# A three-layer compressed interaction network on one core: first layer's sums on ScalarE, first loads on two queues, squares first

## The reference, cut to what matters

```python
e = jnp.stack([tbl_f[ids[:, f]] for f in range(32)], axis=1)     # (2048, 32, 16)
x0, xk, outs = e, e, []
for W in (W0, W1, W2):                                           # (32, Hk, 64), Hk = 32, 64, 64
    xk = relu(einsum('bmd,bhd,mhk->bkd', x0, xk, W))
    outs.append(sum(xk, axis=2))                                 # over d, 16 wide
z = concatenate(outs, axis=1)                                    # (2048, 192)
h = relu(concatenate([z, dense_ctx], 1) @ W_top1 + b_top1)       # 208 -> 512
h = relu(h @ W_top2 + b_top2)                                    # 512 -> 256
y = h @ W_top3                                                   # 256 -> 1
```

## Time and profile before

| | us |
|---|---|
| median of 3 runs | 1193.18 (1192.31 to 1193.81) |
| the profiled execution | 1192.97 |
| its span, first to last instruction | 1191.2 |
| busy: PE / DVE / POOL / ACT | 1121.3 / 1118.8 / 918.8 / 733.9 |
| PE idle at L600, ended by DVE's first-layer products (L556) | 41.6 |
| PE idle at L600, ended by DVE's products (L516) | 21.8 |
| mean time of an `xb` relu (L317), an output relu (L357), a sum (L543) | 0.564, 0.598, 0.776 |

### The profile page before, as it was taken

One profiled execution on the slowest core, in us unless ns is written; L12 is line 12 of the kernel. 1 busy time (PEld: TensorE's weight loads), 2 busy tenths in 40 slices (PEclk: granted clock), 3 DMA queues, 4 the chain that ended last, 5 costly groups with the idle time before them and its releaser, 6 DMA issues.

```text
span 1191.2 us, 14658 instructions
## 1 busy us (share of the span) xinstructions
PE 1121.3 (94%) x5312; PEld 393.6 (33%) x5312; DVE 1118.8 (94%) x521; ACT 733.9 (62%) x1361; POOL 918.8 (77%) x640
## 2 busy tenths in 40 slices
PE   0488899999999999999999999999999999999997
PEld 0122223333333333333333333333333333333333
DVE  0487999999999999999999999999999999999995
ACT  0343666676667667665766766576676657657653
POOL 6688888888888888888888888888888888885400
PEclk9888999999999999999999999999999999999999
DMA  5887787667678766677876666788666778876300
GB/s 110 190 176 146 158 171 155 138 132 144 140 157 171 157 141 141 132 144 150 172 163 136 143 134 145 144 171 168 139 140 134 143 145 169 166 144 144 61 1 1
DMA packets 76216, 167.25 MB, mean 140 GB/s; under 512 B 21776, under 2 KB 39072, under 8 KB 76144
## 3 DMA queue, kind: packets, MB, share of 16 engines
q1 hardware_dynamic: 59216, 161.95, 64.8%
q0 software_dynamic: 16384, 4.23, 3.6%
q10 hardware_dynamic: 544, 0.14, 0.1%
HBM read 157.86 MB, written 8.40 MB: 140 GB/s over the span
## 4 chain that ended last, share of the span: by engine, by line
PE 86%; POOL 3%; DVE 3%; DMA 3%; issue 3%; ACT 1%; SPq 1%; DVEq 0%
PE acc L600 80%; POOL x_rows L254 3%; DVE p_dve L516 3%; PE acc L672 3%; PE acc L658 1%; PE acc L660 1%; DMA q_tile<-x_of_steps 1%; ACT xb L317 1%; DMA x_rows<-in_table,ids_s 1%; PE acc L680 1%; DMA spread<-x_of_steps 1%; SPq L192 1%; DMA x_of_steps<-x_rows 0%; SPq L219 0%; DVE z L543 0%
## 5 line engine op out<-in xcount | busy, mean ns | idle before, releaser
L600 PE MATMUL acc<-p_dve,w_s 128*64 128x512 f32 x3840 | 863.2, 598 | 22.5 <-DVE p_dve L516 21.8
L254 POOL DMA_INDIRECT x_rows<-in_table,ids_s x512 | 493.7, 964 | 146.1 <-issue 131.2
L516 DVE TENSOR_TENSOR p_dve<-spread,xb 128x3072 f32<-128x3072 f32 (+2 forms) x224 | 572.2, 2682 | 2.9 <-issue 2.9
L516 DVE TENSOR_TENSOR p_dve<-spread,xa 128x2048 f32<-128x2048 f32 (+1 forms) x192 | 501.5, 2730 | 16.6 <-issue 9.1
L600 PEld LDWEIGHTS acc<-p_dve,w_s 128*64 128x64 f32 x3840 | 267.9, 137 | 571.5 <-issue 467.2
L317 ACT ACTIVATE xb<-acc 32x512 f32<-32x512 f32 x512 | 288.8, 564 | 71.6 <-DVE p_dve L516 65.5
L266 POOL TENSOR_TENSOR p_l<-spread,q_tile 128x2048 f32<-128x2048 f32 x60 | 272.7, 4573 | 11.0 <-DMA q_tile<-x_of_steps 10.4
L308 ACT ACTIVATE xa<-acc 64x512 f32<-64x512 f32 x256 | 145.9, 570 | 189.6 <-PE acc L600 155.0
L277 POOL TENSOR_TENSOR p_pool<-spread,x_s 128x1024 f32<-128x1024 f32 x64 | 152.2, 2378 | 94.7 <-PE acc L600 45.9
L600 PE MATMUL acc<-p_l,w_s 128*64 128x512 f32 (+1 forms) x640 | 152.5, 612 | 41.6 <-DVE p_l L556 41.6
L326 ACT ACTIVATE x_s<-acc 64x512 f32<-64x512 f32 x256 | 151.5, 592 | 8.3 <-ACT y_row L449 4.8
(11 more groups left out here) (18 smaller groups left out, 151.1 us busy)
## 6 DMA issues: line engine op xcount, KB each, us to landing
spread<-x_of_steps SPq DMA_DIRECT2D x248, 512.0 KB, 17.4
q_tile<-x_of_steps SPq DMA_DIRECT2D x128, 128.0 KB, 11.4
x_rows<-in_table,ids_s POOLq DMA_INDIRECT x512
x_of_steps<-x_rows SPq DMA_DIRECT2D x64, 128.0 KB
spread<-x_of_steps SPq DMA_DIRECT2D x16, 256.0 KB, 5.4
w_s<-in_w SPq DMA_DIRECT2D x2, 512.0 KB, 5.7
wt<-in_w_top SPq DMA_DIRECT2D x1, 512.0 KB, 6.5
z_all<-in_dense_t ACTq DMA_DIRECT2D x16, 8.0 KB, 8.2
```

Of the source, the lines that this page charges most:

```text
L254: nc.gpsimd.indirect_dma_start(out=x_rows[:, s % 2, i * DIM:(i + 1) * DIM], out_offset=None, in_=table, in_offset=bass.IndirectOffsetOnAxi ...
L516: nc.vector.tensor_tensor(p_dve[:, to:to + n, :], spread[:, s % 3, tile:tile + n, :], over(x[:], n), ALU.mult).then_inc(dve_made, n)
L600: last = nc.tensor.matmul(acc[b * K:(b + 1) * K, :], w, prod[:, b * BLK:(b + 1) * BLK], start=start, stop=stop)
```

## The change

1. `out_0` and VectorE's sum of the first layer go. In their place `sums_0` on ScalarE reads acc0 in 32 ACTIVATEs of 128 x 16, each with an accumulator output that is the sum over d, written to `z`. It stands behind x1_b(s). The waits of TensorE for `out_ready[0]` become waits for `z_made[0]`.
2. In steps 0 and 1 `load_q` and `load_a` are shared: SP issues quads 0 and 1, ScalarE quads 2 and 3 (`load_q_and_a`), tile by tile, each tile with its own semaphore. Step 0's `load_b` is shared too; step 1's isn't. VectorE makes those steps' first-layer products in four instructions of one chunk. ScalarE issues step 0's before squares(0) and step 1's behind x1_b(0), ahead of sums_0(0).
3. TensorE's first layer begins with the squares' chunk.
4. out_2(s - 2) comes after x2_a(s - 1). squares(2) comes after x2_b(0) instead of before it.
5. mlp1 and mlp2 come after chunk 8 instead of chunk 5 of layer 1.

```diff
-MLP1_AFTER, MLP2_AFTER, MLP3_AFTER = 5, 5, 13
+MLP1_AFTER, MLP2_AFTER, MLP3_AFTER = 8, 8, 13
...
                 if s < 2:
-                    load_tiles(s, 0, NA // 2, half_a_loaded[s])
-                    load_tiles(s, NA // 2, NA - NA // 2, a_loaded[s])
+                    for i in range(NA - 1):
+                        load_tiles(s, i, 1, tile_loaded[s][i], SP_QUADS)
+                    load_tiles(s, NA - 1, 1, a_loaded[s], SP_QUADS)
...
-                load_tiles(s, NA, NT - NA, b_loaded[s % 3])
+                load_tiles(s, NA, NT - NA, b_loaded[s % 3], SP_QUADS if s == 0 else range(Q))
...
-            def out_0(s):
+            def sums_0(s):
                 if s > 0:
                     act.wait_ge(z_made[0], s)
-                nc.scalar.activation(out_l[:, 0, :], acc0[:], ACT.Relu).then_inc(out_ready[0], 1)
+                if s % 2 == 0 and s >= 4:
+                    act.wait_ge(z_moved, s // 2 - 1)
+                for i in range(SB // 2):
+                    cols = slice(i * DIM, (i + 1) * DIM)
+                    last = nc.scalar.activation(out_l[:, 0, cols], acc0[:, cols], ACT.Relu,
+                                                accum_out=z[:, s // 2 % 2, 0, s % 2, i:i + 1])
+                last.then_inc(z_made[0], 1)
...
+            def load_q_and_a(s):
+                act.wait_ge(x_stored, 32 * (s + 1))
+                if s >= 1:
+                    act.wait_ge(l0_made, CP * s)
+                    act.wait_ge(squares_made, s)
+                for q in ACT_QUADS:
+                    act.dma_start(q_tile[q * FIELDS:(q + 1) * FIELDS, :],
+                                  scratch[s, 0:FIELDS, :]).then_inc(q_loaded, 16)
+                for i in range(NA - 1):
+                    load_tiles(s, i, 1, tile_loaded[s][i])
+                load_tiles(s, NA - 1, 1, a_loaded[s])
             load_dense(0)
+            load_q_and_a(0)
+            load_tiles(0, NA, NT - NA, b_loaded[0])
             act.wait_ge(w_loaded, LOADED)
             squares(0)
             x1_a(0)
             x1_s(0)
-            out_0(0)
             for s in range(STEPS):
...
                 x1_b(s)
+                if s == 0:
+                    load_q_and_a(1)
+                sums_0(s)
+                if s >= 1:
+                    x2_a(s - 1)
                 if s >= 2:
                     out_2(s - 2)
-                if s >= 1:
-                    x2_a(s - 1)
-                if s + 1 < STEPS:
+                if s != 1 and s + 1 < STEPS:
                     squares(s + 1)
...
                     x2_b(s - 1)
+                if s == 1:
+                    squares(2)
...
                     x1_s(s + 1)
-                    out_0(s + 1)
...
-                for c in 0, 2:
-                    if c == 2:
+                for c in range(CP):
+                    if c < CP - 1:
+                        dve.wait_ge(tile_loaded[s][c], 16 * Q)
+                    else:
                         dve.wait_ge(a_loaded[s], 16 * Q)
-                    nc.vector.tensor_tensor(p_l0[:, c:c + 2, :], spread[:, s % 3, c:c + 2, :],
-                                            over(q_tile[:], 2), ALU.mult).then_inc(l0_made, 2)
+                    nc.vector.tensor_tensor(p_l0[:, c, :], spread[:, s, c, :], q_tile[:],
+                                            ALU.mult).then_inc(l0_made, 1)
...
                     if c == NT:
-                        sums(s, 0)
...
-                for c in range(C0):
+                for c in CP, *range(CP):
                     rows = P if c < CP else FIELDS
-                    if c == 0 and s > 0:
+                    if c == CP and s > 0:
                         pe.wait_ge(x1b_ready, s)
-                        pe.wait_ge(out_ready[0], s)
+                        pe.wait_ge(z_made[0], s)
```

More of the change, by code:

```diff
@@ L32 @@
 RING = 10
+SP_QUADS, ACT_QUADS = (0, 1), (2, 3)
 H1, H2 = 512, 256
@@ L137, in build_kernel @@
         q_loaded = sem("q_loaded")
-        half_a_loaded = [sem(f"half_a{s}_loaded") for s in range(2)]
+        tile_loaded = [[sem(f"tile{i}_of_step{s}_loaded") for i in range(NA - 1)] for s in range(2)]
         a_loaded = [sem(f"a_loaded{u}") for u in range(3)]
@@ L153, in build_kernel @@
         x2b_ready = sem("x2b_ready")
-        out_ready = [sem(f"out{n}_ready") for n in range(3)]
+        out_ready = [sem(f"out{n}_ready") for n in (1, 2)]
         z_made = [sem(f"z{n}_made") for n in range(3)]
@@ L184, in store_x, with load_tiles @@
                     sp.dma_start(dst, x_rows[:, s % 2, :]).then_inc(x_stored, 16)
-            def load_tiles(s, first_tile, n, signal):
-                for q in range(Q):
+            def load_tiles(s, first_tile, n, signal, quads=range(Q)):
+                for q in quads:
                     o = Q * first_tile + q + 1
@@ L217, in load_q @@
                     sp.wait_ge(squares_made, s)
-                for q in range(Q):
+                for q in SP_QUADS if s < 2 else range(Q):
                     sp.dma_start(q_tile[q * FIELDS:(q + 1) * FIELDS, :],
@@ L451, in mlp3, with load_tiles @@
                 act.dma_start(y[:, t * P:(t + 1) * P], y_row[:]).then_inc(y_stored, 16)
+            def load_tiles(s, first_tile, n, signal):
+                for q in ACT_QUADS:
+                    o = Q * first_tile + q + 1
+                    first = scratch[s, o:o + 1, :]
+                    src = bass.AP(first.tensor, first.offset, [[COLS, FIELDS], [Q * COLS, n], [1, COLS]])
+                    act.dma_start(spread[q * FIELDS:(q + 1) * FIELDS, s, first_tile:first_tile + n, :],
+                                  src).then_inc(signal, 16)
+            def load_q_and_a(s):
[3 more added lines that the diff above has]
+                    act.wait_ge(squares_made, s)
+                for q in ACT_QUADS:
+                    act.dma_start(q_tile[q * FIELDS:(q + 1) * FIELDS, :],
[3 more added lines that the diff above has]
+                load_tiles(s, NA - 1, 1, a_loaded[s])
             load_dense(0)
+            load_q_and_a(0)
+            load_tiles(0, NA, NT - NA, b_loaded[0])
             act.wait_ge(w_loaded, LOADED)
@@ L616, in layer0 @@
                         pe.wait_ge(squares_made, s + 1)
-                    contract(acc0, w0_s[0:rows, c, :], p_l0[0:rows, c, :], c == 0, c == C0 - 1
+                    contract(acc0, w0_s[0:rows, c, :], p_l0[0:rows, c, :], c == CP, c == CP - 1
                              ).then_inc(l0_used, 1)
@@ L622, in layer1 @@
                 if c == 0 and s >= 2:
[L623 removed]
+                    pe.wait_ge(out_ready[0], s - 1)
                 if c != POOL_CHUNK:
@@ L636, in layer2 @@
                 if c == 0 and s > 0:
-                    pe.wait_ge(out_ready[2], s)
+                    pe.wait_ge(out_ready[1], s)
                 if c != POOL_CHUNK:
```

12 lines of the change are left out of this document (5 added, 7 removed).

## The result

The changed kernel takes **1381.68 us** (median of 4 runs, 1380.26 to 1382.62), the kernel before 1192.74 (4 runs). The ratio is 1.158, 95% interval [1.156, 1.160]: slower by 189 us, where 11.8 less were forecast, and far outside the range.

What follows compares the result with a forecast made beforehand. DVE was taken to set the step, with PE balanced against it from step 4 on. Terms 7.9 + 1.2 + 2.0 + 0.7 = 11.8 us gave 1181.4 on the median's scale; range 1176 to 1200, the forecast's own 1177 to 1187.

Steps and rivals of the forecast that it cites:

- 16 columns come to 0.22 us: ScalarE's sums_0: each 16-column accumulating ACTIVATE takes 0.22 us, bounds 0.07 and 0.44, so 7.0 us for the 32.
- with 7.0 nothing waits: TensorE's mlp1 and mlp2 leave sums_0 7.8 us, so a row of 7.0 us delays nothing.
- Rival A: sums_0 holds PE over acc0; each microsecond beyond 7.8 lengthens 28 steps: 1205, 1231 or far above; chance 0.20.
- the forecast's case: The main forecast for the whole kernel: 11.8 us gained, 1181.4 on the scale of the median; chance 0.56.
- First steps: Steps 0 and 1, up to DVE's layer 1 of step 2: start at 112.2 instead of 120.06, 7.9 us gained.
- which POOL's gathers set and which stays within 0.7 us: Step 1's loads: they start when the gathered rows are stored, 54.81, a time expected to move by 0.7 us at most.
- Steps 2 and 3: No top network yet, PE has room: DVE's dropped sum saves 0.6 us in each, 1.2 us.
- From step 4 on: PE is the bound; only its 0.18 us wait per two steps goes: 2.0 us taken, bounds 0 and 2.5.
- Rival C: DVE alone was the bound: 0.6 us saved in each of 28 steps, 17 us, giving 1166; chance 0.03.
- The tail: At the end DVE is ahead, so its wait at 1153.17 goes: 0.7 us gained.
- Rival B: Early loads arrive no earlier, since half-size DMAs on two queues share engines: 8.3 us gained, 1184.7; chance 0.17.
- Rival D: A small stall, 0.25 to 0.26 us per ACTIVATE, or an early-step wait that eats the gain: about 1192; chance 0.04.

Runs made afterwards that it cites:

- h1: The changed kernel, unaltered, measured again and undisturbed: 1177.55 us, ratio 0.9876 against the kernel before.
- e2: The changed kernel with 32 plain 16-column ACTIVATEs (no accumulator output) and DVE doing the first-layer sum again, undisturbed: 1203.94 us, ratio 1.0096.
- i1: The changed kernel, unaltered, on another chip, undisturbed: 1178.23 us, ratio 0.9884.
- e1: The changed kernel with one ScalarE relu of acc0 in place of sums_0 and DVE's first-layer sum back, undisturbed: 1186.88 us, ratio 0.9954.
- j3: The kernel before with only the loads of steps 0 and 1 on two queues, disturbed chip: 1195.34 us, ratio 1.0016.
- k3: The changed kernel without the gathers of steps 6 to 31, disturbed chip: 1208.37 us, ratio 1.0141.
- k2: The changed kernel with acc0 first copied to SBUF by one relu, TensorE waiting for that alone, sums reading the copy, disturbed chip: 1289.12 us, ratio 1.0796.
- k1: The changed kernel, unaltered, as control on a disturbed chip: 1380.14 us, ratio 1.1578.
- e4: The changed kernel with acc0 first copied to SBUF by one relu, TensorE waiting for that alone, sums reading the copy, undisturbed: 1177.48 us, ratio 0.9872.
- j1: The changed kernel, unaltered, a fourth time, disturbed: 1375.49 us, ratio 1.1532.

## Why the prediction was wrong, and where it was right

**The step that failed is "16 columns come to 0.22 us"**, 7.0 us for the 32, and with it "with 7.0 nothing waits". The price of a row of 32 was taken as a property of the instructions. It is one as long as they arrive: a pair takes 0.157 us, 5.4 or 5.5 us for 32 (h1), below the forecast 7.0. With gathers running beside them on a disturbed chip the same 64 take 9.5 to 12.2 us in the steps 2 to 29 of the three traces, 11.8 on the mean in the trace on record, or 0.37 for each ACTIVATE. That still lies between the prediction's own bounds, 0.07 and 0.44, but 0.44 was meant for a slower instruction, and the range was worked out with 0.22. No instruction became slower: the median ACTIVATE of the row lasts 185 ns in the trace on record and 292 in h1. What was added is time between them, and the longest row of small ACTIVATEs that the prediction had was the six z_all.

**Rival A's mechanism is what happened.** It said that sums_0 would hold TensorE over acc0 beyond 7.8 us, and that PE would be idle before mlp1 and mlp2. In h1 the limit measures 7.7: sums at 628.63, mlp2 at 636.29. A priced each microsecond beyond it at 28 steps; 26 of them have a long row, 11.8 us on the mean, and that is 4.0 x 26 = 104 us, or 1285. The rest up to 1382 has two large parts that A lacked: TensorE's slow pace after each wait (1.7 + 0.55 us in the step shown; with the wait of 4.3 it makes 6.5, and the step grew from 34.5 to 41.0), and the first steps, 16 us later than before instead of 8 earlier, in which sums of 19.6 and 15.8 us and the late issues on SP add up. The range ended at A's beginning, 1200, though A's own numbers went to 1231 and "far above". With a chance of 0.20 for a rival without an upper end, that was the wrong place to cut.

The Trainium skill's page "VectorE: DVE Perf Modes", section "Two Vector instructions with no wait between them", was weighed for A: on VectorE an accumulator output makes two instructions. The trace agrees, and shows it for ScalarE as well: 1024 ACTIVATE and 1024 ACTIVATION_READ_ACCUMULATOR. That doubling costs 0.157 - 0.065 = 0.09 us for each (h1 against the plain ones of e2, start to start), 2.9 us a row, which the limit of 7.7 covers. What it does besides is to put 64 instructions into the row in place of 32, and from step 1 on, in the trace on record, the gaps begin between the 32nd and the 41st. By the Trainium skill's page "ScalarE: Activation LUTs", section "What ACT_TABLE_LOAD costs", the estimate was 0.11 us for each; measured is 0.065 for a plain one (e2) and 0.157 for a pair (h1).

**Undisturbed, the forecast's case came out, and the sum was 3 us short:** 1177.6 and 1178.2 us against 1181.4, 15 us gained instead of 11.8. Term by term, from h1, whose profiled run took 1174.99:

- *First steps: 7.9 us forecast, 13.1 measured.* DVE's timeline in h1, against the earlier trace rows:

```profile
45.15 7.75 DVE L553 TENSOR_TENSOR p_dve<-spread,xa 128x3072 f32<-128x3072 f32 x3 [4.13 <-ACT xa L311]
...
70.53 7.75 DVE L553 TENSOR_TENSOR p_dve<-spread,xa 128x3072 f32<-128x3072 f32 x3 [3.97 <-issue]
78.20 8.81 DVE L553 TENSOR_TENSOR p_dve<-spread,xb 128x3072 f32<-128x3072 f32 x3
...
106.97 7.75 DVE L553 TENSOR_TENSOR p_dve<-spread,xa 128x3072 f32<-128x3072 f32 x3 [3.50 <-issue]
```

  Step 0 was to begin at 47.1 and began at 45.15. Step 1 was to begin at 74.5 and be held by load_b(1) until 79.5; it began at 70.53 and wasn't held. What had been wrong is "which POOL's gathers set and which stays within 0.7 us": SP stores step 1's rows at 47.72 instead of 52.61 and issues its q_tile at 49.92 instead of 54.81. All of step 1's loads are 4.9 us earlier. Layer 1 of step 2 then starts at 106.97 instead of 112.2; the wait before it is 3.50, forecast 3.0.
- *Steps 2 and 3: 1.2 forecast.* DVE's layer 1 of steps 2 and 3 starts 106.97 and 141.00, 34.03 apart instead of 34.61: right.
- *From step 4 on: 2.0 forecast.* PE paces the kernel: mlp1 stands at 602.11 and 671.16, 69.05 us for two steps, 34.5 each. The wait of 0.18 is gone. Rival C, 34.0 throughout, is out.
- *The tail: 0.7 forecast.* In h1 no wait for DVE's products is left in the last step. From layer 1 of step 2 to the end it is 4.9 us shorter in all, against 3.9 forecast for the three terms; in i1 it is 2.3 (1068.8 instead of 1071.1), so this part varies between runs by as much as a term.
- *That the sums pay:* e1, with DVE's sum back, takes 1186.88, 9 us more than the unaltered kernel. Its first steps are 2.5 us later (109.50 and 106.97) and its steady step 0.1 longer (34.62 and 34.53), so the profiles show some 7 of the 9 (1182.4 and 1174.99). As forecast, most of DVE's 0.6 us a step buys nothing.
- *Rival B* (loads no earlier) is out: DVE starts at 45.15. But on a disturbed chip j3 shows its outcome, with the start at 51.09 and no gain, though for another reason: SP's late issues, not DMAs that share engines.
- *Rival D* (a small stall) is out in h1: PE waits for sums_0 nowhere.

**Shown and open.** Shown: the loss begins with gaps between ScalarE's small instructions, for which the profile has no cause but "issue"; that the supply of instructions runs short is read from their rhythm, and isn't shown by itself. The gaps come where gathers run beside the row and end where the gathers end (k3, and the last two steps of each disturbed trace of the changed kernel); without the wait for acc0 91 us of the loss go (k2 against k1), and of the 111 that k2 keeps over the undisturbed 1178, 30 are in the first steps (layer 1 of step 2 at 137.23 instead of 106.97) and 28 x 2.9 = 81 in the steps of 37.4 us, in which out_2 comes late. Open: what differs between the two kinds of measurement. The gathers take as long in both (a mean of 0.957 and 0.958 us in k1 and h1), the bytes and queues are the same, and one chip number shows both. One rival was not tested, that the loading of the program's code is behind it. The page of the profile lists two DMA queues of the kind "instruction"; they have the same 42 and 45 packets on record and in h1, far fewer than the 296 waits, which speaks against it without excluding it. Not tried: gathers moved out of the way of the sums, the small instructions spread between the long ones of x1_b and x2_a, and e2's 32 plain ones on a disturbed chip, a row that may be short enough.

## What to carry to other kernels

A long row of very short instructions can be limited by something other than their durations, here most likely by how fast they arrive, and no duration in a profile of a kernel without such a row shows that. Look at what a short row would hold up if it took twice as long, and release the shared buffer with one long instruction ahead of it, as e4 does: it cost nothing undisturbed (1177.48 against 1177.6 to 1178.2) and saved 91 us disturbed. The fastest kernels of this study are the changed one and e4, but on a disturbed chip both lose to the kernel before; there the best that was measured is the old way, 1192.5.

## What the runs showed of the hardware that was not expected

- An accumulating ACTIVATE of 16 columns from PSUM and its accumulator read take 0.157 us together, start to start (h1); from SBUF 0.20 (e4); a plain one of 16 columns from PSUM 0.065 (e2).
- With indirect DMAs running, ScalarE's instructions came in groups about 0.7 us apart once some 31 to 40 had gone (28 in the first step), in three of five measurements of one program. 172 us of its 1380 went when the gathers did. SP was late in the same measurements, though no run ties that to the gathers: ten issues took 11.64 us (12.11 in k3, 7.68 in j1) instead of 5.16 (h1).
- A wait of 4.3 us left TensorE at the 1.2 GHz level for the next 5 us (granted clock 0.51); a pause of 2.51 us before the change did not the earlier trace rows. The length of the pause alone doesn't decide it: in the trace on record a pause of 1.92 us, before 147.77, was followed by a granted clock of 0.50 from 148 to 151.
